# Moving the difference sums of the activations from VectorE to GpSimd in a mixture-of-experts kernel

## The reference

```
x = x + softmax(affine(normalised(out @ kv.T)))     # attention block, kv = ctx @ W_k.T + b_k
x = x + moe(layernorm(x))
def moe(x):                                          # 4096 rows of 1024 values
    probs = softmax(x @ gate_w)                      # 8 experts, the best 2 of each row
    topk_w, topk_idx = top_k(probs, 2); topk_w /= sum(topk_w)
    rows sorted by expert                            # 8192 rows in all
    h   = silu(rows @ w1[e]) * (rows @ w3[e])        # 1024 -> 3584
    out = h @ w2[e]                                  # 3584 -> 1024
    return each row's two results, weighted with topk_w and added
```

## Time and profile before

| | |
|---|---|
| time, median of 3 runs | 8154.1 us (8140.57 to 8154.86) |
| profiled execution: time / span | 8154.86 us / 8153.3 us |
| mean granted TensorE clock | 0.972 |
| PE busy | 7728.8 us (95%) |
| DVE busy | 4354.9 us (53%) |
| ACT busy | 2988.2 us (37%) |
| POOL busy | 1842.3 us (23%) |
| chain that ended last | PE 84%, DMA 4%, DVE 2%, issue 2% |

### The profile page before, as it was taken

How to read it: one execution, slowest core, us unless ns; L and a number is a source line. 1 busy time by engine, 2 the same in 40 slices (tenths; PEclk the granted TensorE clock), 3 DMA queues, 4 the chain that set the end, 5 groups by cost and what they waited for, 6 DMA issues and landing times.

```text
span 8153.3 us, 143429 instructions
## 1 busy us (share of the span) xinstructions
PE 7728.8 (95%) x47421; PEld 6903.0 (85%) x47422; DVE 4354.9 (53%) x6365; ACT 2988.2 (37%) x5051; POOL 1842.3 (23%) x1540
## 2 busy tenths in 40 slices
PE   8959999999999999999999999999999999999998
PEld 5538887788789999888779999888778999999997
DVE  6765555555555445555554545555554554545454
ACT  2323334333443334333443334433343333433343
POOL 2333311232112211233103221132112221032211
PEclk8969999999999999999999999999999999999999
DMA  3322236322652235422562225522463225622265
GB/s 114 112 88 73 87 127 198 114 89 84 202 161 71 79 118 182 128 82 84 164 192 74 79 84 183 158 79 89 133 196 101 74 79 166 186 76 74 76 189 157
DMA packets 606830, 979.04 MB, mean 120 GB/s; under 512 B 45152, under 2 KB 281072, under 8 KB 606576
## 3 DMA queue, kind: packets, MB, share of 16 engines
q1 hardware_dynamic: 571696, 902.21, 33.9%
q0 software_dynamic: 34880, 74.14, 4.1%
HBM read 783.93 MB, written 194.35 MB: 120 GB/s over the span
## 4 chain that ended last, share of the span: by engine, by line
PE 84%; DMA 4%; DVE 2%; issue 2%; ACT 1%; SPq 0%; POOL 0%; DVEq 0%; ACTq 0%; POOLq 0%
PE pair L1527 55%; PE pair L1560 28%; DMA raw<-hd 2%; DVE wl L1238 1%; DMA part<-hd 1%; ACT wh L1042 1%; PE pair L1608 1%; DVE hid L1378 0%; PE pair L1627 0%; SPq L978 0%; DMA raw<-in_L_ffn_w 0%; DMA w_last<-in_L_ffn_w 0%; DVE xl L1238 0%; DVE part L1378 0%; DMA part<-x_rows,id_g 0%
## 5 line engine op out<-in xcount | busy, mean ns | idle before, releaser
L1527 PE MATMUL pair<-xh,wh 128*128 128x264 f32 (+3 forms) x9408 | 2513.9, 321 | 94.1 <-issue 53.5
L1527 PE MATMUL pair<-xh,wl 128*128 128x264 f32 (+3 forms) x9408 | 2519.5, 322 | 0.0
L1527 PE MATMUL pair<-xl,wh 128*128 128x264 f32 (+3 forms) x9408 | 2515.5, 322 | 0.0
L1238 DVE TENSOR_TENSOR wl<-raw,wh 128x512 fp32r<-128x512 f32 x2019 | 1452.5, 744 | 1803.5 <-ACT wh L1042 1777.8
L1042 ACT ACTIVATE wh<-raw 128x512 fp32r<-128x512 f32 x2019 | 1215.1, 629 | 1896.8 <-PE pair L1560 1006.5
L1527 PEld LDWEIGHTS pair<-xh,wh 128*128 128x128 f32 x9408 | 1581.7, 190 | 224.0 <-issue 78.2
L1527 PEld LDWEIGHTS pair<-xh,wl 128*128 128x128 f32 x9408 | 1578.0, 189 | 127.8
L1527 PEld LDWEIGHTS pair<-xl,wh 128*128 128x128 f32 x9408 | 1573.0, 189 | 124.4
L1560 PE MATMUL pair<-wl,wh 128*128 128x264 f32 (+3 forms) x5376 | 1452.2, 325 | 0.0
L1560 PE MATMUL pair<-wh,wl 128*128 128x264 f32 (+3 forms) x5376 | 1451.6, 325 | 0.0
L1560 PE MATMUL pair<-wh 128*128 128x264 f32 (+3 forms) x5376 | 1248.5, 328 | 152.2 <-DVE wl L1238 91.8
(11 more groups left out here) (236 smaller groups left out, 4921.0 us busy)
## 6 DMA issues: line engine op xcount, KB each, us to landing
raw<-in_L_ffn_w SPq DMA_DIRECT2D x226, 1024.0 KB, 6.0
raw<-hd SPq DMA_DIRECT2D x672, 272.0 KB, 3.0
raw<-in_L_ffn_w SPq DMA_DIRECT2D x672, 256.0 KB, 2.6
hd<-hid SPq DMA_DIRECT2D x112, 1088.0 KB, 5.1
part<-hd SPq DMA_DIRECT2D x224, 272.0 KB, 3.0
w_last<-in_L_ffn_w SPq DMA_DIRECT2D x224, 256.0 KB, 2.7
xin<-in_x SPq DMA_DIRECT2D x8, 2048.0 KB, 10.4
out_x<-x SPq DMA_DIRECT2D x32, 512.0 KB, 3.0
```

What stands on the lines that cost most here:

```text
L1238: return V.tensor_tensor(out, a, b, ALU.subtract)
L1527: mm = pe.matmul(to[:, c, 0:hi - lo], entry(w, e)[:, ks], x[:, e, k, lo:hi], start=begin and k == 0 and i == 0, stop=k == KH - 1 and i == ...
```

## The change

The difference sums of the activations (`row_sum`), those of the tail (`tail_sums`) and the weight sums of a slot's first tile (`weight_sum`) leave DVE. POOL does them: `row_sums` in one piece after the gather of its pass and before the scatter of the pass before, `tail_sums` behind it in pass 1, and the weight sums in pass 3 before the last scatter, once the activations of all four passes have been read. The same differences are formed, in the same buffers. In front of the first slot the sums move in the same way.

```diff
-            def weight_sum(s, i, a, n):      # on DVE, one sum per call
...
-            def row_sum(n, quads, i):        # on DVE, one difference per call
...
-            def tail_sums(s):                # on DVE
...
                     rows_lo(n + c, c, 0, steady)
                     rows_lo(n + c, c, 1, steady)
-                    row_sum(n + c, steady, 0)
                     steps(t + 4, t + 5)
                     rows_lo(n + c, c, 2, steady)
-                    steps(t + 5, t + 6)
-                    for i in range(1, 4):
-                        row_sum(n + c, steady, i)
-                        steps(t + 5 + i, t + 6 + i) if i < 3 else None
-                    rows_lo(n + c, c, 3, steady)
-                    for i in range(4, EP):
-                        steps(t + 2 * i, t + 2 * i + 2)
+                    for i in range(3, EP):
+                        steps(t + 2 * i, t + 2 * i + 2) if i > 3 else steps(t + 5, t + 8)
                         rows_lo(n + c, c, i, steady)
...
-                        tail_sums(s + 1)
...
-                        for k in range(4):
-                            steps(t + 20 + 2 * k, t + 22 + 2 * k)
-                            weight_sum(s + 1, 0, 0, k)
...
+            def row_sums(n, quads):          # on POOL
+
+                x11, x21, x12, x22 = quads
+                pool.wait_ge(s_quad, n * 4 + 4)
+                pool.wait_ge(s_xlo, n * EP + 1)
+                G.tensor_tensor(x11, x12, x11, ALU.subtract).then_inc(s_xsum, 1)
+                G.tensor_tensor(x12, x22, x12, ALU.subtract).then_inc(s_xsum, 1)
+                pool.wait_ge(s_xsum, n * 4 + 1)
+                pool.wait_ge(s_xlo, n * EP + 3)
+                G.tensor_tensor(x22, x22, x11, ALU.subtract).then_inc(s_xsum, 1)
+                pool.wait_ge(s_xsum, n * 4 + 3)
+                G.tensor_tensor(x21, x21, x22, ALU.subtract).then_inc(s_xsum, 1)
...
+            def tail_sums(s):                # on POOL, the same with tiny
...
                         gather(c + 1, xg, s_xg)
+                    row_sums(s * 4 + 4 + c, steady)
+                    if c == 1:
+                        tail_sums(s + 1)
                     if c > 0:
                         scatter(s, c - 1, width, s * 11 + (10, 12, 13)[c - 1])
+                pool.wait_ge(s_xlo, s * (4 * EP) + 8 * EP)
+                weight_sums(s + 1, 0, 0, fresh=True)
                 scatter(s, 3, width, s * 11 + 14)
                 weight_sums(s + 1, 0, 1)
...
                 gather(c + 2, first_x[c], s_xfirst[c + 2])
+                row_sums(c, first_q[c])
             pool.wait_ge(s_xt, 12)
             tick(3)
             gather_tail(s_xfirst[4])
+            for c in (2, 3):
+                row_sums(c, first_q[c % 2])
+            tail_sums(0)
             pool.wait_ge(s_xlo, 4 * EP)
```

More of the change, by code:

```diff
@@ L1241, in plus @@
                 return V.tensor_tensor(out, a, b, ALU.add)
-            def weight_sum(s, i, a, n):
[L1245 to L1258, removed]
-            def row_sum(n, quads, i):
[L1262 to L1275, removed]
-            def tail_sums(s):
[L1279 to L1282, removed]
-                less(x12, x22, x12).then_inc(s_tsum, 1)
-                dve.wait_ge(s_tsum, s * 4 + 1)
-                less(x22, x22, x11).then_inc(s_tsum, 1)
-                dve.wait_ge(s_tsum, s * 4 + 3)
-                less(x21, x21, x22).then_inc(s_tsum, 1)
             def weight_lo(s, i, a, e):
@@ L1484, in _ @@
             for c in range(4):
-                for i in range(3):
+                for i in range(EP):
                     rows_lo(c, c, i, first_q[c % 2])
-                for i in range(4):
-                    row_sum(c, first_q[c % 2], i)
-                for i in range(3, EP):
-                    rows_lo(c, c, i, first_q[c % 2])
-            for i in range(3):
-                tail_lo(0, i)
-            tail_sums(0)
-            for i in range(3, EP):
+            for i in range(EP):
                 tail_lo(0, i)
@@ L1726, in weight_sums @@
                 G.tensor_tensor(sums[:, 3, :, :], A12, sums[:, 2, :, :], ALU.subtract).then_inc(s_sum, 1)
+            def row_sums(n, quads):
[10 more added lines that the diff above has]
+            def tail_sums(s):
+                x11, x21, x12, x22 = (tail(q) for q in range(4))
+                pool.wait_ge(s_tq, s + 1)
+                pool.wait_ge(s_tlo, s * EP + 1)
+                G.tensor_tensor(x11, x12, x11, ALU.subtract).then_inc(s_tsum, 1)
+                G.tensor_tensor(x12, x22, x12, ALU.subtract).then_inc(s_tsum, 1)
+                pool.wait_ge(s_tsum, s * 4 + 1)
+                pool.wait_ge(s_tlo, s * EP + 3)
+                G.tensor_tensor(x22, x22, x11, ALU.subtract).then_inc(s_tsum, 1)
+                pool.wait_ge(s_tsum, s * 4 + 3)
+                G.tensor_tensor(x21, x21, x22, ALU.subtract).then_inc(s_tsum, 1)
             def records(s):
```

4 lines of the change are left out of this document (1 added, 3 removed).

## The result

| | before | after |
|---|---|---|
| time, median us (range, runs) | 8147.3 (8133.4 to 8154.9, 4) | 8203.0 (8200.3 to 8223.4, 4) |
| ratio to before, 95% interval | 1 | 1.0079 (1.0058 to 1.0099) |
| profiled execution, time / span us | 8154.86 / 8153.3 | 8231.72 / 8230.1 |
| mean granted TensorE clock | 0.972 | 0.973 |

The changed kernel is slower, by 56 us between the medians; the forecast was 8185 us, 31 more than before. The ratio goes by two more executions of the changed kernel (8218.6 and 8231.7 us) than the four of the table, and so comes out above 8203.0 / 8147.3. Its profiled execution was 28.7 us above its own median, so the two traces differ by more (76.8 us of span) than the two medians. Sums over the traces are therefore held against 77 us, and ratios against 0.79%.

A forecast was written before the change was run, and what follows sets the result against it. PE was taken to bound the kernel, busy 7728.8 of 8153.3 us. Terms 0 + 53 - 87 + 48 + 8 + 8 = +30 us gave 8185 us; the forecast's own range was 8165 to 8215, 8 in 10 8105 to 8250.

The forecast's parts named there:

- the two mechanisms: Down phase: POOL's sums alternate with DVE's low parts, +53 us; the scatter moves from pass starts to mid-pass, -87 and +48.
- differences leave DVE: Down phase: 2.7 us of DVE work per pass sits in gaps that exist, so removing it is worth 0.
- they come onto POOL: Steps 3 to 5 of the down phase: POOL's differences delay DVE's low parts, 43 us, plus 10 for half-clock steps.
- scatter leaves the pass starts: Steps 2 to 4 of passes 1 to 3: loads take 3.0 us again, -87 us.
- scatter at its new places: Near step 6 in passes 2 and 3, step 16 in pass 1: 2.0 us per scatter, +48 us.
- weight sums, tail: Pass 3, steps 13 to 15: weight sums alternate with DVE, half hidden by a load wait, +8 us; tail's cost nothing.
- before the first slot: Ahead of slot 0: the last high part starts 3 us later, four quarters +12, shorter end -4, +8 us.
- the extra step at half clock: Behind the longer gaps at step 4: half of 12 bring a half-clock step of 1.7 us, 10 us more.
- the rival of the costly scatter: Scatter costs 4.2 us mid-pass as at pass starts, 100 us in place of 48: +82 us, 8237 us; chance 0.16.
- The faster case: Scatter costs only 0.6 us at its new place, sums fit DVE's gaps: -49 us, 8106 us; chance 0.27.
- Nothing happens: Slack of loads and DVE swallows both, contention under 0.5 us a pass: about 8155 us; chance 0.15.

The follow-up runs named there:

- the last experiment: Kernel before, sums on DVE, scatter issued late in passes 1 and 2 only, at its old place in pass 3; ratio 0.9991.
- the one with the spare writes: Kernel before, scatter DMAs pointed out of bounds, plus four write-only POOL instructions a pass and two tiny sums; ratio 0.9900.

## Why the prediction was right, and what in it was mis-sized

The sign, the two mechanisms and the places were right. The time came out near the top of the forecast's own range of 8165 to 8215, and the ratio (1.0079, at least 1.0058) above the forecast's 1.0038: the loss was about twice the one forecast, and it is the width of the range that holds it. Term by term, the traces in us:

| term | predicted | shown by | measured |
|---|---|---|---|
| differences leave DVE | 0 | late scatter, sums on DVE: no loss at steps 2 to 4 | 0 |
| they come onto POOL | +43, and +10 for the clock | scatter off, DVE against POOL | +50 |
| scatter leaves the pass starts | -87 | late scatter alone | -86 |
| scatter at its new places | +48 | kernel after, less before, from step 5 on | +105 |
| weight sums, tail | +8 | weight sums back on DVE | 0, not to be told from 8 |
| before the first slot | +8 | start of the trace | +8 |
| sum | +30 | | +77 |

*No loss from DVE's own differences.* Right: with the scatter away from the starts and the sums on DVE, steps 2 to 4 of passes 1 to 3 lose 0.1 us at most. The load was the cause of the old gap, not DVE. The spare time was read too large, though: PE begins some 0.4 us after the end of the low part that it waits for (1342.03 and 1342.44 in the kernel after), so of the 0.56 us between 1170.04 and 1170.60 only about 0.15 were in hand.

*POOL beside DVE.* The step as worked out, 1.16 + 0.6 + 1.16 + 0.65 us from the end of the second `xl` piece, is in the trace: step 4 was to come 1.9 us late and came 2.0 late. Without scatter traffic, the cost by pass is 1.2, 1.5, 2.0 and 1.5 us in the mean of all slots, against 1.1 and 1.9 in narrow slots and 0.8 and 1.1 in wide ones. In wide slots the gap at step 4 was 1.3 instead of 1.1, in narrow ones 1.6 to 2.0, and the extra step at half clock came in two of the 12 longer gaps of the narrow slots (in the kernel after in one), against half of them in the prediction. The errors nearly cancel, so 50 us measured against 53 is partly luck. That pass 0 lost at step 5 was right too (about 1.2 us in narrow slots, 0.7 in wide ones). Slot 7, with 3.70 us between the starts of steps 4 and 5 instead of 2.95; the timelines of DVE, POOL and PE:

```profile
7835.39 2.68 DVE L1238 TENSOR_TENSOR wl<-raw,wh 128x512 fp32r<-128x512 f32 x2 [0.95 <-ACT wh L1042]
...
7834.52 1.29 POOL L1672 TENSOR_TENSOR sums<-sums 128x512 f32<-128x512 f32 x1 [3.14 <-DVE xl L1238]
7835.89 1.62 POOL L1674 TENSOR_TENSOR sums<-sums 128x512 f32<-128x512 f32 x1
...
7838.22 0.48 PE L1495 MATMUL pair<-wh 128*128 128x264 f32 x2 [0.64 <-DVE wl L1238]
```

The prediction gave the hold by the Trainium skill's word (page "SBUF — State Buffer": the second to issue "fully blocks"; section "Who interferes with whom" has these words of DVE's 2-port modes, section "Summary: rules for kernel authors" of two SBUF inputs beside a GpSimd instruction that reads SBUF as well) as a whole POOL instruction, and by the earlier trace rows as 1.16 us. In the trace after, DVE's first low part starts 0.49 us behind POOL's first difference, of which 1.19 us are left, and takes 1.73 us, 1.04 more than alone. So the hold is the rest of a POOL instruction, a whole one only where the two start together, and both descriptions fit.

*The scatter's new places.* This is the term that was mis-sized: "24 x 2.0 = +48 us". In the kernel after, less before, it cost 2.9 us a scatter in pass 2 (steps 5 to 12), 3.4 in pass 1 (steps 13 to 27) and 6.8 in pass 3 (steps 5 to 12), in all 23 + 27 + 54 = 105 us with rounding, 4.4 in the mean of 24. The 2.0 came from the 1 MB weight loads of pass 3, as the nearest rows, with 1.7 us each; where a scatter meets no such load it is still 1.4 to 1.7 times the 2.0. Pass 3 was worse because I placed the scatter near step 6 and the first weight load at step 6 and priced them as if they met PE one at a time. They come within 0.13 us of each other, and the small loads behind the 1 MB load in SP's queue take 11.05 us. Separating them by two steps or more took 0.50% off with the sums on DVE (0.24% with them on POOL, which is not clear of noise), and leaving pass 3 alone took off all of the late scatter's loss. That shows that the meeting costs; how the DMA engines share their time between the three was not looked into. The prediction had this meeting only in the rival of the costly scatter, at 4.2 us for all 24; it is 6.8 for eight of them and about 3 for sixteen.

*Something that no term held.* A gap at the pass start may also shelter what follows. With the scatter's traffic gone and no gap at the starts, the weight loads of pass 3, the first of them clean before but for slots 1 and 5, cost 3.2 us a slot at steps 5 to 12 (1.3 before) and 3.7 further on (1.9 before): (1.9 + 1.8) x 8 = 30 us given back later. On one chip, with the sums on DVE, the last experiment (a gap of 3.5 at the start of pass 3) has 1.1 and 3.0 us there, and the one with the spare writes (no gap) 3.3 and 3.7, some 22 us in all. So part of the 54 us in pass 3 is not the scatter's; (8.1 - 3.2) x 8 = 39 is. But with the sums on POOL the shelter hardly shows: scatter first, with the largest gap at the start of pass 3 (4.8), loses 2.7 and 2.8 us there, and without scatter it is 3.4 and 2.5. These readings are from the excess by steps of single traces; that there is a shelter, and how it would work (an interval of rest in which the loads get ahead), was not tested.

*Weight sums.* They alternate with DVE's low parts as said. By the excess at steps 13 to 27 of pass 3 the wait vanishes wholly in that of the second weight load, not by half; the ratios (1.0079 and 1.0086) can't tell.

*Before the first slot.* +3.0 us a quarter as worked out, and a shorter end: from PE's first instruction of this stretch to the first unit 59.0 us against 51.1, +8. The untouched part of the program ahead of it happened to be 5.8 us shorter in that execution, and the stretches between the down phases 4 us, which is why the traces don't show these 8 in their difference; and the 11 us of the slower median step are in no term. That the sum meets 77 so closely is therefore partly luck.

*The rivals.* The faster case asked for scatters of 0.6 us; no mean of a pass, here or in the experiments, is below 2.6. The round-robin rule of the Trainium skill ("DMA: Bandwidth & Descriptors", section "Queues, rings and completion order"), by which a load beside a scatter should keep half its rate, would have given 6 us for a load of 3.0; the loads in pass 2 take 4.4 to 4.9 and fit it, that of 11.05 us in pass 3 does not, and its place behind 1 MB in the same queue has to be counted as well. "Nothing happens" fell with both mechanisms shown.

## What to carry to other kernels

Work that an engine does in its idle time costs nothing where it is (0 us here), and moving it to a neighbour that reads through the same port can cost something (50 us here): look for instructions with two SBUF inputs on DVE beside anything on POOL that reads SBUF, and price each meeting as the rest of POOL's instruction. Whatever is queued behind the moved work moves too; ask of each DMA that slides which other transfer it now meets, and price that meeting as one event, not as two. And a gap that disappears may have been the cover of the next one, so add nothing up before looking at what follows it.

## What the runs showed of the hardware that was not expected

- Work on POOL whose result nobody uses costs 0.55% of the kernel's time when it reads SBUF (4 x 32 subtractions of 1.34 us, 172 us in all, for about 45 us of time) and nothing when it only writes (128 of 0.36 us); a low part of DVE takes up to 1.56 us beside such a read, 0.69 at most beside such a write.
- POOL pays too: its difference of 128x512 takes 1.60 to 1.66 us in the mean beside DVE's low parts, 1.27 to 1.29 where nothing holds it up.
- Five scatter DMAs let out in four portions cost more than a burst in passes 1 and 2, 4.4 to 4.6 us a pass against 2.8 to 3.8, and less than a burst that meets a weight load in pass 3, 5.5 against 9.1.
- Small loads of 256 and 272 KB took 9.5 and 11.05 us when a 1 MB load ahead of them in SP's queue and a scatter ran together; 3.0 is the median before.
- All scatter traffic of the experts together, 24 scatters inside the down phases and 8 behind them, is worth 0.99% of the time with the sums on DVE (0.9901), about 80 us.
